# Group mean of y taken off by the product that turns y back to token order, and the centred tile copied by ScalarE, in a macaron block on one core

## The chip, the core and the metric

The kernel runs on one core of one Trainium2 chip. The time is device microseconds (us) of one execution of the whole program. The engines are TensorE (PE in the profile; its weight loads are PEld), VectorE (DVE), ScalarE (ACT), GpSimd (POOL) and SyncE (SP), which issues the DMAs. Each engine works through its own instructions in the order in which they are written, and waits on semaphores for the others.

## What is computed

The input x is 1024 tokens by 256 channels, all fp32. The block is x + 0.5 ffn(layernorm(x)), then + retention(layernorm(x)), then + 0.5 ffn(layernorm(x)) again. The change lies in the retention part:

```python
y = jnp.einsum('bhts,bhsd->bhtd', scores, v)
yg = y.transpose(0, 2, 1, 3).reshape(B * T, H, D)        # H = 16 groups of D = 16
mu = jnp.mean(yg, axis=-1, keepdims=True)
var = jnp.var(yg, axis=-1, keepdims=True)
yn = (yg - mu) / jnp.sqrt(var + EPS)
yn = yn.reshape(B * T, C) * gn_weight[None] + gn_bias[None]
out = jax.nn.silu(x @ w_g) * yn
return out @ w_proj
```

Each token has 16 groups of 16 neighbouring channels, and each group loses its own mean.

## The kernel before

The tokens are cut into 8 chunks of 128 (NT = 8), the channels into 2 halves of 128 (KC = 2). The first feed-forward part, the retention part and the second feed-forward part follow each other and overlap at their edges. No scheduler stands between the text and the chip: each engine has one block in which its steps are called in the order in which they run.

The retention part runs as a loop over c = 0 to 6, with the steps of several chunks in one iteration, and a written-out ending for chunk 7. On PE an iteration is: scores(c), project_out(c-3), project_vg(c+1), turn_h2(c+2), values(c, 0), turn_gn(c-2), values(c, 1), turn_qk(c+1), turn_y(c-1), project_qk(c+2), update_state(c+1). The ending is turn_h(2), turn_y(6), scores(7), project_out(4), values(7, 0), values(7, 1), turn_gn(5), turn_y(7), gate_up(12) and so on; gate_up starts the second feed-forward part. So turn_y(0) to turn_y(5) are called in the loop, and turn_y(6) and turn_y(7) behind it.

For one chunk the group norm goes through these steps:

- PE's values (L1107, L1101) leaves y in PSUM with the channels in partitions; ACT's copy_y (L458) copies it to yT in SBUF.
- PE's turn_y (L1140) turns it to token order by two transposes of 128x128 into the first 256 columns of bank 7 (bank 5 for chunk 7).
- DVE's group_mean sums each group (gsum, L735) and subtracts gsum/16 from the turned tile (gd, L739, into SBUF; gd has two buffers).
- ACT's square (L465) makes gsq, DVE's group_var (L747) sums it to gvar, POOL's group_roots makes gve (L320) and the power -0.5, grstd (L324), DVE's group_norm (L753) makes gn.
- PE's turn_gn (L1153) turns gn into the other half of the same bank, ACT's affine (L473) makes ga, DVE's gated (L761) go, PE's project_out (L1163) the product, and DVE's add_proj (L765) adds it to x1.

Other names in the rows: turn_qk is L1068, project_qk L1042, update_state L1120, scores L1085, project_vg L1053 and L1056, turn_h2 L1030, turn_h L961, gate_up L986. ACT's copy_qk makes kT (L446), qM (L448, two instructions) and qT (L452); copy_v makes v (L433) and sg (L437). DVE's rotate_parts makes rc and rs (L695), mask_kv kvm (L725), mask_scores sc (L715, four instructions), rotate rot (L707, L708), fuse_up fuse (L660), norm_tile h (L632), rest_h hh (L644).

Two guards matter for the order. turn_y(c) writes the bank from which the centred tile of the chunk before is read, so turn_y(6) waits for gd_done of chunk 5; turn_gn(c) and project_out(c) wait for gd_done of later chunks that share the bank. The constants (identity, causal mask, group mask and two columns) come in one tile msk by one DMA, which SP issues behind the first weight pieces and the first half of x.

Of the kernel before, what the change touches and what calls it, by code (L numbers as in the profile page):

```python
# [27 lines left out]
ALU = mybir.AluOpType  # L28
# [75 lines left out]
def masks():  # L104

    p = np.arange(P)
    return np.concatenate([
        np.eye(P), p[:, None] <= p[None, :], p[:, None] // D == p[None, :] // D,
        (p[:, None] // D) % 2 == np.arange(2)[None, :],
    ], 1).astype(np.float32)  # L110


def macaron(nc, x, w_qkv, w_g, w_proj, gn_w, gn_b, gate_w, up_w, down_w, gate_s, up_s, down_s,
            rotation_t, mask_t, out):
    with ExitStack() as ctx:
        def sb(name, shape, dt=F32):
            return ctx.enter_context(nc.sbuf_tensor(name, shape, dt))

        def sem(name):
            return ctx.enter_context(nc.semaphore(name))  # L120
# [11 lines left out]
        msk = sb("msk", [P, 3 * P + 2])  # L132
# [28 lines left out]
        gsum = sb("gsum", [P, H])  # L161
# [15 lines left out]
        ident, causal, own = msk[:, 0:P], msk[:, P:2 * P], msk[:, 2 * P:3 * P]  # L177
        gate_col, up_col = vec[:, 0:NI], vec[:, NI:2 * NI]
# [12 lines left out]
        def packed(ring, q):  # L191
# [39 lines left out]
        yT_done, y_turned, gsum_done, gd_done, gsq_done, gvar_done, gve_done, grstd_done, gn_done = (  # L231
            sem(n) for n in ("yT_done", "y_turned", "gsum_done", "gd_done", "gsq_done", "gvar_done", "gve_done",
# [143 lines left out]
        def _(act):  # L376
# [16 lines left out]
            def split_h(g, k):  # L393

                act.wait_ge(turned, (g if g < NG else g + NG) * TH + TH)
                if g >= NG:
                    act.wait_ge(up_done, NG * NI)
                nc.scalar.activation(hhi[:, k, g % NG, :], turn[g][k][:, :], ACT.Copy).then_inc(hhi_done, 1)
# [61 lines left out]

            def square(c):
                act.wait_ge(gd_done, c + 1)
                if c >= 1:
                    act.wait_ge(gvar_done, c)
                nc.scalar.activation(gsq[:, :], gd[:, c % 2], ACT.Square).then_inc(gsq_done, 1)  # L465
# [61 lines left out]
            for c in range(NT - 1):  # L527
                if c >= 2:
                    square(c - 2)
                copy_v(c + 1)  # L530
                if c + 2 < NT:
                    copy_h2(c + 2)
                if c >= 2:
                    affine(c - 2)
                copy_y(c)
                copy_qk(c + 1)
            c, j0 = NT - 1, NG * NI
            square(c - 2)
            split_h(2, 0)
# [3 lines left out]
            affine(c - 2)  # L543
            square(c)
# [23 lines left out]
        def _(dve):  # L568
# [162 lines left out]
            def group_mean(c):  # L731
                dve.wait_ge(y_turned, c + 1)
                if c >= 1:
                    dve.wait_ge(gd_done, c)
                dve.tensor_reduce(gsum[:, :], per_head(b_turned_y[c][:, 0:C]), AX.X, ALU.add).then_inc(gsum_done, 1)  # L735
                dve.wait_ge(gsum_done, c + 1)
                if c >= 2:
                    dve.wait_ge(gn_done, c - 1)
                dve.scalar_tensor_tensor(out=per_head(gd[:, c % 2]), in0=gsum[:, :].unsqueeze(2).to_broadcast([P, H, D]),  # L739
                                         scalar=-1.0 / D, in1=per_head(b_turned_y[c][:, 0:C]),  # L740
                                         op0=ALU.mult, op1=ALU.add).then_inc(gd_done, 1)

# [114 lines left out]
            for c in range(NT - 1):  # L857
# [21 lines left out]
                if c >= 1:  # L879
                    group_mean(c - 1)  # L880
# [6 lines left out]
            group_mean(c - 1)  # L887
# [8 lines left out]
            group_mean(c)  # L896
# [42 lines left out]
        def _(pe):  # L939
# [184 lines left out]
            def turn_y(c):  # L1124
# [14 lines left out]
                for k in range(KC):  # L1139
                    mm = pe.transpose(b_turned_y[c][:, k * P:(k + 1) * P], yT[:, c % 2, k, :], ident)  # L1140
# [142 lines left out]
```

## Time and profile before

| what | value |
|---|---|
| median of 3 runs | 173.49 us (173.36 to 173.67) |
| the profiled execution | 173.6 us |
| its span, first to last instruction | 171.8 us |
| mean granted TensorE clock | 0.999 |
| PE, DVE, ACT, POOL busy | 161.0, 137.1, 75.9, 68.9 us |

The span is 1.8 us shorter than the time of the same execution. A row of the timeline gives start, duration, engine, line, operation, output <- input, and how often it stands there in a row; square brackets give the engine's idle time before it and what ended that. The chain of waits is followed back from the last instruction; in it a PE row lasts only until the next instruction of PE starts, so its numbers are the pace at which PE moves on. In the timeline a PE row holds the whole pipeline of its last instruction too, and rows overlap.

### The profile page before, as it was taken

The numbers are of one execution on the slowest core, as the hardware profiler recorded it, in microseconds if no ns is written. First come the engines' busy times: TensorE is split into PE (matmuls) and PEld (weight loads), VectorE is DVE, ScalarE is ACT, GpSimd is POOL, SyncE is SP. The second block draws the span as 40 slices with busy tenths as digits, with TensorE's granted clock in tenths as the row PEclk, the third lists the DMA queues.
The fourth block names the chain that finished last, engine by engine and source line by source line (L and its number), as shares of the span: only waits on it lengthen the run. The fifth ranks groups of instructions, "written<-read, shape, count | busy, mean of one in ns | idle before, by whom it ended". The sixth has DMA issues, their size and how long they took to land.

```text
span 171.8 us, 3264 instructions
## 1 busy us (share of the span) xinstructions
PE 161.0 (94%) x1125; PEld 123.1 (72%) x1125; DVE 137.1 (80%) x294; ACT 75.9 (44%) x162; POOL 68.9 (40%) x76
## 2 busy tenths in 40 slices
PE   5996998989989999999999999999899999999992
PEld 2454766678969786768686777867666788898881
DVE  2799989999847266869797979998887899666763
ACT  3145398869402306161707062534716646225600
POOL 2354295425580611117474746465297530000000
PEclk9999999999999999999999999999999999999999
DMA  4999203803000000000000000000000000011002
GB/s 155 277 352 310 84 2 64 306 0 120 4 0 0 4 0 0 4 0 0 6 0 4 2 0 0 4 0 6 0 0 2 0 4 0 0 61 61 6 31 92
DMA packets 6848, 8.41 MB, mean 49 GB/s; under 512 B 416, under 2 KB 5552, under 8 KB 6832
## 3 DMA queue, kind: packets, MB, share of 16 engines
q1 hardware_dynamic: 6832, 8.20, 14.9%
q8 instruction: 9, 0.15, 0.4%
q14 instruction: 7, 0.06, 0.1%
HBM read 7.15 MB, written 1.05 MB: 48 GB/s over the span
## 4 chain that ended last, share of the span: by engine, by line
PE 62%; DVE 19%; issue 7%; POOL 6%; DMA 3%; ACT 2%; SPq 0%; POOLq 0%; DVEq 0%
PE bank L986 18%; PE bank L1014 10%; PE bank L1042 7%; PE bank L1107 5%; POOL grstd L324 3%; PE bank L1053 3%; PE bank L1085 3%; PE bank L1056 3%; PE bank L1163 3%; DVE h L632 3%; DMA xt<-in_L_attn_x 3%; PE bank L1068 2%; DVE fuse L660 2%; DVE sc L715 2%; DVE grid L574 2%
## 5 line engine op out<-in xcount | busy, mean ns | idle before, releaser
L986 PE MATMUL bank<-hh,gate_r 128*128 128x512 f32 x96 | 27.6, 407 | 2.5 <-DVE hh L644 1.0
L986 PE MATMUL bank<-hh,up_r 128*128 128x512 f32 x96 | 26.3, 396 | 0.0
L1014 PE MATMUL bank<-down_r,fhi 128*128 128x256 f32 x96 | 24.3, 291 | 0.3 <-DVE flo L668 0.3
L324 POOL TENSOR_TENSOR grstd<-gve,neg_half 128x16 f32<-128x16 f32 x8 | 23.3, 2917 | 0.7
L1014 PE MATMUL bank<-down_r,flo 128*128 128x256 f32 x96 | 23.4, 282 | 0.0
L408 ACT ACTIVATE gact<-bank,vec 128x512 f32<-128x512 f32 x24 | 16.4, 685 | 14.9 <-PE bank L986 14.6
L986 PEld LDWEIGHTS bank<-hh,gate_r 128*128 128x128 f32 x96 | 16.8, 188 | 8.0 <-issue 3.7
L660 DVE SCALAR_TENSOR_TENSOR fuse<-bank,vec,gact 128x512 f32<-128x512 f32 x24 | 17.9, 745 | 4.1 <-PE bank L986 3.9
L986 PEld LDWEIGHTS bank<-hh,up_r 128*128 128x128 f32 x96 | 18.1, 188 | 4.3
L715 DVE TENSOR_TENSOR sc<-bank,msk 128x512 f32<-128x512 f32 x32 | 19.8, 680 | 0.0
L433 ACT ACTIVATE v<-bank 128x256 f32<-128x256 f32 x8 | 3.1, 384 | 37.0 <-PE bank L1056 37.0
L1014 PEld LDWEIGHTS bank<-down_r,fhi 128*128 128x128 f32 x96 | 18.1, 188 | 1.5 <-DVE flo L668 1.0
L1014 PEld LDWEIGHTS bank<-down_r,flo 128*128 128x128 f32 x96 | 18.1, 188 | 0.5 <-issue 0.2
L416 ACT ACTIVATE fhi<-fuse 128x512 fp32r<-128x512 f32 x24 | 14.9, 629 | 6.8 <-DVE fuse L660 6.8
L1042 PE MATMUL bank<-wqkv,h 128*128 128x512 f32 x32 | 15.1, 594 | 0.0
L668 DVE TENSOR_TENSOR flo<-fuse,fhi 128x512 fp32r<-128x512 f32 x18 | 13.3, 744 | 0.8 <-ACT fhi L416 0.7
L678 DVE TENSOR_TENSOR yd<-bank,ds 128x256 f32<-128x256 f32 x16 | 6.7, 422 | 8.5 <-PE bank L1014 8.4
L1107 PE MATMUL bank<-sc,v 128*32 128x128 f32 x256 | 13.1, 279 | 0.0
L300 POOL TENSOR_SCALAR ve<-mv 128x1 f32<-128x1 f32 (+3 forms) x14 | 3.8, 272 | 23.0 <-DVE mv L607 22.9
L293 POOL TENSOR_TENSOR grid<-raw,grid 128x256 f32<-128x256 f32 (+2 forms) x6 | 7.7, 1290 | 12.3 <-DVE raw L586 12.3
L308 POOL TENSOR_TENSOR flo<-fuse,fhi 128x512 fp32r<-128x512 f32 x6 | 9.6, 1611 | 4.9 <-ACT fhi L416 4.9
L302 POOL TENSOR_TENSOR rstd<-ve,neg_half 128x1 f32<-128x1 f32 (+3 forms) x14 | 10.0, 715 | 1.2
(80 smaller groups left out, 300.0 us busy)
## 6 DMA issues: line engine op xcount, KB each, us to landing
raw<-in_rotation SPq DMA_DIRECT2D x1, 1536.0 KB, 7.1
xt<-in_L_attn_x SPq DMA_DIRECT2D x2, 512.0 KB, 5.4
out<-xt SPq DMA_DIRECT2D x8, 128.0 KB, 1.7
raw<-in_L_ffn_down_w SPq DMA_DIRECT2D x2, 384.0 KB, 8.2
wqkv<-in_L_attn_w_qkv SPq DMA_DIRECT2D x1, 768.0 KB, 9.6
raw<-in_rotation SPq DMA_DIRECT2D x1, 512.0 KB, 3.5
raw<-in_L_ffn_gate_w SPq DMA_DIRECT2D x1, 384.0 KB, 7.2
raw<-in_L_ffn_up_w SPq DMA_DIRECT2D x1, 384.0 KB, 7.7
```

What stands on the lines that cost most here:

```text
L302: pool.tensor_tensor(rstd[:, a:b], ve[:, a:b], neg_half[:, 0:b - a], ALU.pow).then_inc(rstd_done, 1)
L308: pool.tensor_tensor(flo[:, g % NG, i, :], fuse[:, j % FUSE_SLOTS, :], fhi[:, g % NG, i, :].bitcast(F32), ALU.subtract).then_inc(flo_pool, 1)
L324: pool.tensor_tensor(grstd[:, c % 2], gve[:, :], neg_half[:, :], ALU.pow).then_inc(grstd_done, 1)
L408: nc.scalar.activation(gact[:, j % 2, :], pairs[j // (NG * NI)][j % 2][0][:, :], ACT.Silu, scale=gate_col[:, i:i + 1]).then_inc(silu_done, 1)
L416: nc.scalar.activation(fhi[:, g % NG, i, :], fuse[:, j % FUSE_SLOTS, :], ACT.Copy).then_inc(fhi_done, 1)
L660: dve.scalar_tensor_tensor(out=fuse[:, j % FUSE_SLOTS, :], in0=pairs[j // (NG * NI)][j % 2][1][:, :], scalar=up_col[:, i:i + 1], in1=gact[ ...
L668: dve.tensor_tensor(flo[:, g % NG, i, :], fuse[:, j % FUSE_SLOTS, :], fhi[:, g % NG, i, :].bitcast(F32), ALU.subtract).then_inc(flo_dve, 1)
L715: dve.tensor_tensor(sc[:, r].rearrange("p k m t -> p (k m) t"), b_sc[r][:, :].rearrange("p (g t) -> p g t", t=P), causal.unsqueeze(1).to_b ...
L986: mm = pe.matmul(dst[:, :], wr[m][:, k * I + i * P:k * I + (i + 1) * P], half[:, k, g % NG, :], start=(k == 0 and half is hhi), stop=(k == ...
L1014: mm = pe.matmul(downs[d][:, 0:C], half[:, g % NG, i, t * P:(t + 1) * P], wr["down"][:, i * C:(i + 1) * C], start=(i == 0 and half is fhi) ...
L1042: mm = pe.matmul(b_qk[:, :], h2[:, c % 2, k, :], wqkv[:, k, 0:2 * C], start=(k == 0), stop=(k == KC - 1))
L1107: mm = pe.matmul(b_y[r * 2 * D:(r + 1) * 2 * D, k * P:(k + 1) * P], v2[:, c % 2, hd, :], sc[:, r, k, m, :], start=(c == 0 and m == 0), sto ...
```

## The change

The constant tile gets a fourth 128x128 matrix, named centre: identity minus 1/16 wherever row and column belong to one group. turn_y multiplies yT by it (an ordinary fp32 product) where it was transposed with the identity, so that the turned tile comes out with each group's mean taken off. DVE's group_mean and the tile gsum go. ACT's new step copy_centred copies the turned, centred tile from PSUM to gd; it is called at the end of each iteration of the loop and twice in the ending.

```diff
 def masks():
         (p[:, None] // D) % 2 == np.arange(2)[None, :],
+        np.eye(P) - (p[:, None] // D == p[None, :] // D) / D,
...
-        msk = sb("msk", [P, 3 * P + 2])
+        msk = sb("msk", [P, 4 * P + 2])
...
+        centre = msk[:, 3 * P + 2:]
...
+            def copy_centred(c):
+                act.wait_ge(y_turned, c + 1)
+                if c >= 2:
+                    act.wait_ge(gn_done, c - 1)
+                    act.wait_ge(gsq_done, c - 1)
+                nc.scalar.activation(gd[:, c % 2], b_turned_y[c][:, 0:C], ACT.Copy).then_inc(gd_done, 1)
...
                 copy_y(c)
                 copy_qk(c + 1)
+                if c >= 1:
+                    copy_centred(c - 1)
             c, j0 = NT - 1, NG * NI
             square(c - 2)
+            copy_centred(c - 1)
             split_h(2, 0)
             split_h(2, 1)
             square(c - 1)
             copy_y(c)
             affine(c - 2)
+            copy_centred(c)
             square(c)
...
-            def group_mean(c):
-                dve.wait_ge(y_turned, c + 1)
-                if c >= 1:
-                    dve.wait_ge(gd_done, c)
-                dve.tensor_reduce(gsum[:, :], per_head(b_turned_y[c][:, 0:C]), AX.X, ALU.add).then_inc(gsum_done, 1)
-                dve.wait_ge(gsum_done, c + 1)
-                if c >= 2:
-                    dve.wait_ge(gn_done, c - 1)
-                dve.scalar_tensor_tensor(out=per_head(gd[:, c % 2]), in0=gsum[:, :].unsqueeze(2).to_broadcast([P, H, D]),
-                                         scalar=-1.0 / D, in1=per_head(b_turned_y[c][:, 0:C]),
-                                         op0=ALU.mult, op1=ALU.add).then_inc(gd_done, 1)
...
                     gated(c - 2)
-                if c >= 1:
-                    group_mean(c - 1)
...
             c, j0 = NT - 1, NG * NI
-            group_mean(c - 1)
             group_var(c - 2)
...
             rest_h(2, 1)
-            group_mean(c)
...
                 for k in range(KC):
-                    mm = pe.transpose(b_turned_y[c][:, k * P:(k + 1) * P], yT[:, c % 2, k, :], ident)
+                    mm = pe.matmul(b_turned_y[c][:, k * P:(k + 1) * P], yT[:, c % 2, k, :], centre, start=True, stop=True)
                 mm.then_inc(y_turned, 1)
```

The order of PE's steps is the same in both kernels. ACT, at the end of an iteration of the loop (here c = 5) and the start of the next, before the change:

```order
L446 ACTIVATE kT<-bank 128x256 [waits sc_done,qk_turned]
L448 ACTIVATE qM<-bank,msk 128x2x128 x2
L452 ACTIVATE qT<-bank 128x256 [waits y_half]
L465 ACTIVATE gsq<-gd 128x256 [waits gvar_done,gd_done]
L433 ACTIVATE v<-bank 128x8x2x16 [waits y_half,kv_done,vg_done]
```

The same place after the change, where line numbers have moved:

```order
L447 ACTIVATE kT<-bank 128x256 [waits sc_done,qk_turned]
L449 ACTIVATE qM<-bank,msk 128x2x128 x2
L453 ACTIVATE qT<-bank 128x256 [waits y_half]
L467 ACTIVATE gd<-bank 128x256 [waits gsq_done,gn_done,y_turned]
L473 ACTIVATE gsq<-gd 128x256 [waits gvar_done,gd_done]
L434 ACTIVATE v<-bank 128x8x2x16 [waits y_half,kv_done,vg_done]
```

The copy to gd stands between the copies of q and k and the square; before, gd came from DVE, beside those copies.

DVE, from the last norm tile of the loop to the masks of chunk 7 and the norm of chunk 5, before the change:

```order
L632 TENSOR_SCALAR h<-x,mv,rstd 128x256 [waits turned,rstd_done]
L761 TENSOR_TENSOR go<-ga,sg 128x256 [waits proj_done,sg_done,ga_done]
L735 TENSOR_REDUCE gsum<-bank 128x16 [waits gd_done,y_turned]
L739 SCALAR_TENSOR_TENSOR gd<-gsum,bank 128x256 [waits gn_done,gsum_done]
L735 TENSOR_REDUCE gsum<-bank 128x16 [waits gd_done,y_turned]
L739 SCALAR_TENSOR_TENSOR gd<-gsum,bank 128x256 [waits gn_done,gsum_done]
L747 TENSOR_REDUCE gvar<-gsq 128x16 [waits gve_done,gsq_done]
L715 TENSOR_TENSOR sc<-bank,msk 128x512 [waits y_half,sc_done] x4
```

The same place after the change:

```order
L644 TENSOR_SCALAR h<-x,mv,rstd 128x256 [waits turned,rstd_done]
L761 TENSOR_TENSOR go<-ga,sg 128x256 [waits proj_done,sg_done,ga_done]
L747 TENSOR_REDUCE gvar<-gsq 128x16 [waits gve_done,gsq_done]
L727 TENSOR_TENSOR sc<-bank,msk 128x512 [waits y_half,sc_done] x4
L747 TENSOR_REDUCE gvar<-gsq 128x16 [waits gve_done,gsq_done]
```

The sum of squares of chunk 5 (the first gvar) now stands right behind go, with the four instructions for the means of chunks 5 and 6 gone from ahead of it.

ACT in the ending, after the change:

```order
L473 ACTIVATE gsq<-gd 128x256 [waits gvar_done,gd_done]
L467 ACTIVATE gd<-bank 128x256 [waits gsq_done,gn_done,y_turned]
L399 ACTIVATE hh<-bank 128x512 [waits up_done,turned] x2
L473 ACTIVATE gsq<-gd 128x256 [waits gvar_done,gd_done]
L459 ACTIVATE yT<-bank 128x256 [waits y_turned,y_half]
L481 ACTIVATE ga<-bank,vec 128x128 [waits go_done,gn_turned]
L467 ACTIVATE gd<-bank 128x256 [waits gsq_done,gn_done,y_turned]
```

Before the change the same stretch read gsq, hh twice, gsq, yT, ga; the copies of chunks 6 and 7 are put between these.

## Rows read from the trace of the kernel before

**Rows 1.** The page: busy time, share of the span, instructions

```profile
PE 161.0 (94%) x1125; PEld 123.1 (72%) x1125; DVE 137.1 (80%) x294; ACT 75.9 (44%) x162; POOL 68.9 (40%) x76
```

**Rows 2.** Busy time in one iteration: PE, PEld, DVE, ACT, POOL, clock, DMA, GB/s

```profile
93.44:102.52 9.08, 9.08 (x87) 6.80 (x86) 7.78 (x18) 3.82 (x12) 4.93 (x5) 1.00 0.00 1
```

**Rows 3.** Chain of waits (start, us, what): one iteration, pace of PE's steps

```profile
91.41 0.37 PE bank L1153 x2
...
92.60 0.58 PE bank L1068 x4
93.19 0.22 PE bank L1140 x2
93.40 1.72 PE bank L1042 x4
95.12 0.45 PE bank L1120 x4
```

**Rows 4.** Groups by line: what goes from DVE, and ACT's copy from PSUM

```profile
L735 DVE TENSOR_REDUCE gsum<-bank 128x16 f32<-128x256 f32 x8 | 3.4, 422 | 3.8 <-PE bank L1140 3.8
L739 DVE SCALAR_TENSOR_TENSOR gd<-gsum,bank 128x256 f32<-128x256 f32 x8 | 3.4, 421 | 0.3
...
L458 ACT ACTIVATE yT<-bank 128x256 f32<-128x256 f32 x8 | 3.1, 384 | 6.8 <-PE bank L1107 6.5
```

**Rows 5.** Timeline: ACT and DVE in one iteration of the loop

```profile
94.21 0.39 ACT L452 ACTIVATE qT<-bank 128x256 f32<-128x256 f32 x1
...
94.94 0.42 DVE L747 TENSOR_REDUCE gvar<-gsq 128x16 f32<-128x256 f32 x1 [0.30 <-ACT gsq L465]
95.28 0.68 DVE L695 TENSOR_TENSOR rc<-bank,raw 128x512 f32<-128x512 f32 x1
...
99.49 0.38 ACT L433 ACTIVATE v<-bank 128x256 f32<-128x256 f32 x1 [4.58 <-PE bank L1056]
...
99.53 0.41 DVE L753 TENSOR_TENSOR gn<-gd,grstd 128x256 f32<-128x256 f32 x1
...
100.42 0.20 PEld L1153 LDWEIGHTS bank<-msk,gn 128*128 128x128 f32 x2 [0.20 <-issue]
```

**Rows 6.** Timeline: the ending up to the second values of chunk 7

```profile
121.41 0.39 ACT L452 ACTIVATE qT<-bank 128x256 f32<-128x256 f32 x1
...
122.17 0.41 PE L1140 MATMUL bank<-msk,yT 128*128 128x128 f32 x2 [0.70 <-issue]
...
122.51 1.15 PE L1085 MATMUL bank<-qM,kT 32*128 32x256 f32 x16
...
123.41 0.41 DVE L747 TENSOR_REDUCE gvar<-gsq 128x16 f32<-128x256 f32 x1
123.74 2.48 DVE L715 TENSOR_TENSOR sc<-bank,msk 128x512 f32<-128x512 f32 x4
...
126.13 0.41 DVE L747 TENSOR_REDUCE gvar<-gsq 128x16 f32<-128x256 f32 x1
...
127.28 0.20 POOL L320 TENSOR_SCALAR gve<-gvar 128x16 f32<-128x16 f32 x1 [0.16 <-POOL grstd L324]
```

**Rows 7.** Timeline: where TensorE waits for the norm of chunk 6

```profile
127.56 3.00 POOL L324 TENSOR_TENSOR grstd<-gve,neg_half 128x16 f32<-128x16 f32 x1
...
128.66 1.16 PE L986 MATMUL bank<-hh,gate_r 128*128 128x512 f32 x4
...
131.08 0.44 PE L1153 MATMUL bank<-msk,gn 128*128 128x128 f32 x2 [0.32 <-DVE gn L753]
```

**Rows 8.** Chain of waits: pace of a pair of gate and up products

```profile
135.86 1.86 PE bank L986 x8
```

**Rows 9.** DMA issues: out<-in, KB each, us to landing

```profile
msk<-in_masks SPq DMA_DIRECT2D x1, 193.0 KB, 4.4
```

**Rows 10.** Timeline: TensorE waits for DVE at the start

```profile
9.06 0.13 PEld L1173 LDWEIGHTS bank<-msk,rows 16*128 16x128 f32 x1 [0.76 <-issue]
...
11.37 1.08 PE L961 MATMUL bank<-msk,h 128*128 128x128 f32 x6 [0.37 <-DVE h L632]
```

More of the change, by code:

```diff
@@ L160, in macaron @@
         yT = sb("yT", [P, 2, KC, P])
-        gsum = sb("gsum", [P, H])
         gd = sb("gd", [P, 2, C])
@@ L230, in macaron @@
             sem(n) for n in ("sc_done", "sc_masked", "y_half", "kv_done", "kvm_done", "state_done"))
-        yT_done, y_turned, gsum_done, gd_done, gsq_done, gvar_done, gve_done, grstd_done, gn_done = (
-            sem(n) for n in ("yT_done", "y_turned", "gsum_done", "gd_done", "gsq_done", "gvar_done", "gve_done",
+        yT_done, y_turned, gd_done, gsq_done, gvar_done, gve_done, grstd_done, gn_done = (
+            sem(n) for n in ("yT_done", "y_turned", "gd_done", "gsq_done", "gvar_done", "gve_done",
                              "grstd_done", "gn_done"))
```

## The prediction, made before the changed kernel ran

> **What bounds the kernel now.** I read the busy shares first [rows 1]: TensorE is busy for 94% of the span, VectorE 80%, ScalarE 44%. A share of the whole doesn't say what one step is worth, so I then asked for the busy time of one iteration of the retention loop [rows 2]. There TensorE is busy 9.08 us of 9.08, VectorE 7.78 and ScalarE 3.82. The reader is to see that the two engines which the change relieves and loads both have slack in the loop, and the third has none. The chain of waits says the same in another way [rows 3]: through the loop it runs over TensorE alone, one step ending where the next begins, and turn_y is one of these steps. From this follows the frame of the whole estimate: a step on TensorE counts in full in the loop, one on VectorE or ScalarE counts only if it makes TensorE wait. Behind the loop, from 111 to 135 us, this is different: there TensorE waits several times [rows 6, 7], and I go through these waits one by one. Behind 135.4 us the chain is again TensorE's, until the last product of gate and up.
>
> **The product in the place of the transpose.** The two transposes of one turn_y move TensorE on by 0.22 us, 0.11 each [rows 3]. An fp32 product of the same shape stands in the same iteration: update_state multiplies a 128x128 tile by 128 columns, twice. In the chain that is x4 and 0.45 us, where the two transposes were x2 and 0.22 [rows 3]. So an fp32 product is two instructions of TensorE at the pace of one transpose each, and the new turn_y should stand in the trace as x4 and 0.45: 0.22 us more. That holds at both ends of the pace, since both rows are read back to back in a busy stretch.
> In the loop turn_y is called six times. Five of them (chunks 0 to 4) are followed by project_qk without a wait: 5 x 0.22 = **+1.10 us**. The sixth is followed by turn_h and then by turn_y(6), where TensorE was idle for 0.70 us [rows 6]; that idle time takes it.
> The Trainium skill speaks against the change more strongly. Its page "TensorE: Matmul & The Clock Gate", section Terms, calls the transpose mode four times as fast for FP32. By that rule the new turn_y would take 0.88 us, and the five would cost 3.3 us and not 1.1. The rows of this case show two times, and the sum goes by them.
>
> **VectorE's mean.** Eight times 422 + 421 ns go [rows 4], 6.7 us of VectorE's work. In the loop this is worth nothing by itself, because TensorE doesn't wait for VectorE there: gn ends at 99.94 and TensorE loads it at 100.42 [rows 5]. In the ending it can matter (below).
>
> **ScalarE's copy.** It reads PSUM and writes 128x256 in SBUF, as the copy to yT does in 384 ns [rows 4]: 8 x 0.38 = 3.1 us on an engine that then waits 4.58 us for the next chunk's v [rows 5]. Its place is what has to be followed. It is queued behind qT, which starts at 94.21 and takes 0.39 [rows 5]. One after the other, qT, the copy (0.38) and the square (taken like a copy) bring gvar to 94.21 + 0.39 + 0.38 + 0.38 = 95.36, or 0.1 us less or more for overlaps and semaphores. Before, it was at 94.94. TensorE's own 0.22 us delays everything behind turn_y, but not the q and k copies ahead of it; against TensorE's next steps gvar is thus late by 0.42 - 0.22 = 0.2 us. Queued behind gvar on VectorE are rc, rs, the mask of kv and the four masks of scores, then gn and rot. All move by the same 0.2 us, since gvar gave way to rc within 0.34 us before. The nearest user is turn_gn: gn had 0.48 us in hand [rows 5], of which 0.28 remain. I take nothing for the loop. If the cover were gone, TensorE would wait once per iteration from c = 2 to 5.
> The waits that copy_centred adds are on y_turned, which turn_y sets at about 93.19 + 0.45 = 93.64 [rows 3], 0.9 us before the copy's turn, and on gn and gsq of earlier chunks, which are an iteration old.
>
> **The ending.** Times here are on the clock of before, shifted by the 1.10 us.
> turn_y(6) waited until gd of chunk 5 was there (122.17) [rows 6]. The copy to gd is queued behind qT, which starts at 121.41: it ends at 121.41 + 0.39 + 0.38 = 122.18 at the latest, so turn_y(6) starts where it did, and the sixth 0.22 is absorbed. It is longer itself, so scores(7) start 0.2 later. They took until 123.66, and the masks began at 123.74 [rows 6]: now 123.9. **+0.2 us**, for values(7) wait for these masks.
> turn_y(7) is longer too, **+0.22 to 0.25**. So gate_up(12), at 128.66 before [rows 7], starts at 129.1.
> Then comes the join with the norm of chunk 6. Before, the power on GpSimd for this chunk ended at 130.56 and turn_gn(6) started at 131.08 [rows 7]. A pair of gate and up products takes 1.86 [rows 8], so TensorE had come to that point at 130.52 and stood for 0.56 us (0.32 in the row, which counts the end of the pipeline; that is the other bound). Now gvar of chunk 5 no longer waits for the means of 5 and 6 on VectorE (123.41 before [rows 6]; now one more 0.38 behind the copy, about 122.6), so GpSimd's power for chunk 5 ends before gvar of chunk 6 arrives. That one stands behind the masks, at 126.3 and not 126.13; gve, which began at 127.28 behind the previous power [rows 6], begins at 126.8, the power ends at about 130.1, and turn_gn(6) could start at 130.6. TensorE arrives at 129.1 + 1.86 = 130.96. The wait is gone and TensorE itself is next: 130.96 against 131.08 is **-0.12 us** for the ending as a whole, +0.12 by the other bound. The last join, gn of chunk 7, is gated by fuse on VectorE behind gate_up(13), so it follows TensorE.
>
> **The start.** The tile msk grows by 128 x 128 x 4 bytes = 64 KB. Its DMA took 4.4 us for 193 KB [rows 9]; in proportion that would be at most 1.5 us more. The first use is at 9.06, and TensorE then waits for h from VectorE at 11.37 all the same [rows 10]. I take 0, since that wait lies between; the upper bound would leave up to 1 us.
>
> **The sum.** +1.10 for the loop, -0.12 for the ending, 0 for the start: +1.0 us. The profiled execution took 173.6 with a span of 171.8, so I expect a span of 172.8 and 174.6 for such an execution. The median of the runs is 0.1 below it: **174.5 us**.
>
> **Rivals.**
> *The loop now waits for the group norm as well.* If the chain qT, copy, gsq, gvar is slower than I put it (0.5 us against TensorE where I put 0.2), gn comes 0.2 to 0.25 us too late for turn_gn in four iterations, and the ending is later by as much: +1.0 + 0.9 = about 175.5. For it speaks that only 0.28 us remain. Against it, that each of the four durations has its row.
> *Freed VectorE pays: the kernel gets faster.* turn_gn advances TensorE by 0.37 where two transposes need 0.22, and turn_qk by 0.58 for four where 0.44 would do [rows 3]. If these gaps came from VectorE's queue, a VectorE with 0.84 us less per iteration would close them; with the like of project_out some 0.5 us in each of four iterations, 2.0 - 1.0: 172.5. It decides from 0.25 us per iteration on. Against it: gn was ready 0.48 us before its use [rows 5], and the profile names no releaser for the gap.
> *It costs nothing that can be measured.* The ending gives back 0.7 us more: the power of chunk 6 ends 0.5 earlier, and if gate_up(12) weren't in front of turn_gn(6), that would reach the end. Then +0.3 or less: 173.8. Against it: the order of TensorE's steps is fixed, and gate_up(12) is ahead.
> *The product costs four transposes.* That is the skill's rule, worked as a mechanism of this kernel: 0.66 us for each of the five, and 1.3 in the ending less the 0.56 wait: +4.0, 177.6. Against it stands update_state with its own row [rows 3].
>
> **How the numbers follow.** A difference of 0.2% (0.35 us) is about what can be told from no change here. My forecast (between +0.6 and +1.4) gets 0.68, the late norm 0.12, four transposes 0.02, no measurable change 0.10, faster 0.08. Slower by over 0.2% is thus 0.82, within it 0.10, faster 0.08. The forecast's own spread is the ending's 0.25 us, the pace (0.22 or 0.23) and some 0.2 us at the start. The range has to take in the late norm at the top, and comes down to just where a change can't be measured at the bottom: 173.8 to 175.6.
>
> **What would show it.** Right: turn_y as x4 and 0.45 in the chain, x32 in all, an iteration of 9.30 us with TensorE full; gvar about 0.2 us later against rc's producer; the second power in the ending about 0.5 us earlier, and TensorE's 0.32 us before turn_gn(6) gone. Wrong: a wait of TensorE on gn inside the loop; an iteration of 9.08 or less; turn_h's products at 11.37 later by more than 0.1 us.

## The result, and the profile after

The changed kernel takes 174.34 us (median of 7 runs, 174.19 to 184.25), the kernel before 172.99 us in the same comparison. The ratio is 1.0071, 95% interval 1.0049 to 1.0092: slower, by 1.2 us. Forecast were 174.5 us and +1.0 us against the kernel before. That the time itself lies so near the forecast is in part luck: the kernel before took 172.99 us here, where the forecast started from 173.49, and the loss was larger than forecast.

The profiled execution of that comparison ran at a granted clock of 0.856 and took 184.25 us; it is left out of the ratio, as three executions of 389 to 855 us are in the comparisons further down. The rows below are from a second run of the same changed kernel with a clock of 1.000 (174.32 us, span 172.5). Its page first: busy time, share of the span, instructions.

```profile
PE 162.1 (94%) x1141; PEld 124.7 (72%) x1141; DVE 131.5 (76%) x278; ACT 79.0 (46%) x170; POOL 69.5 (40%) x76
```

Beside [rows 1]: TensorE has 16 instructions more (eight turn_y's with two more each) and 1.1 us more busy time, VectorE 16 instructions and 5.6 us less, ScalarE 8 instructions and 3.1 us more. VectorE is relieved by five times what TensorE is loaded with, and the kernel is slower.

Where it went shows in the busy time of two iterations of the loop (columns as in [rows 2]: the stretch, then PE, PEld, DVE, ACT, POOL). The first is the second iteration, the other a full one, each from one project_qk to the next.

```profile
75.25:84.22 8.97, 8.97 (x87) 6.63 (x85) 6.36 (x15) 4.21 (x13) 5.15 (x5) 1.00 0.01 2
93.53:102.84 9.31, 9.31 (x91) 7.04 (x89) 7.04 (x16) 4.21 (x13) 5.20 (x6) 1.00 0.01 3
```

The full iteration is 9.31 us where it was 9.08 [rows 2]. TensorE shows no idle time in either; a wait shorter than the 0.28 us that a row of one product lasts doesn't show as idle time, as the second iteration will tell. The chain of waits of the changed kernel in a full iteration answers [rows 3]:

```profile
91.47 0.37 PE bank L1149 x2
...
92.66 0.59 PE bank L1064 x4
93.25 0.45 PE bank L1136 x4
93.69 1.72 PE bank L1038 x4
95.41 0.45 PE bank L1116 x4
```

turn_y (L1136) is now x4 and 0.45, to the digit what update_state (L1116) is. The other steps are as they were, the 0.37 of turn_gn and the 0.59 of turn_qk included.

I measured all kernels in the same way, since the starts of TensorE's steps repeat to 0.02 us between two profiles of one kernel. The table has the iterations from the start of one project_qk to that of the next, their sum, and the time from the last project_qk to turn_gn(7), behind which every kernel has 36.4 us left. The first start counted is that of project_qk(2), the first one that the loop calls; the iteration named the second is that of c = 2, and the last iteration of the loop, c = 6, lies in the ending.

| kernel | iterations, us | sum | ending |
|---|---|---|---|
| before, two profiles | 8.29, 8.54, 9.08, 9.08, 9.08 | 44.07 | 24.02 |
| changed, two profiles | 8.52, 8.97, 9.31, 9.31, 9.31 | 45.42 | 23.96 |
| product_alone | 8.51, 8.69, 9.31, 9.31, 9.31 | 45.13 | 24.30 |
| copy_alone | 8.29, 8.97, 9.08, 9.08, 9.08 | 44.50 | 23.85 |
| v_centred | 8.29, 8.97, 9.07, 9.08, 9.08 | 44.49 | 23.84 |
| product_square_first, two profiles | 8.52, 8.69, 9.31, 9.31, 9.31 | 45.14 | 23.83 |
| v_square_first, two profiles | 8.29, 8.52, 9.08, 9.08, 9.08 | 44.05 | 23.40 |
| reduced_product | 8.24, 8.97, 9.08, 9.09, 9.08 | 44.46 | 23.92 |
| double_copy | 8.52, 9.24, 9.36, 9.35, 9.35 | 45.82 | 24.50 |

The changed kernel loses 1.35 us in the loop and gets 0.06 back in the ending: 1.29 us. Four of the five iterations lose 0.23 each. The second loses 0.43, and that is the one thing the forecast did not have.

How well whole times can be told apart has to be said once. The span of one kernel varies by 0.9 us between executions (before: 171.0 to 171.9 in one comparison, with one at 172.5), and the loop's first project_qk, project_qk(2), of the same changed kernel starts at 66.73 in one profile and 67.18 in another. The two profiles of before, at 67.33 and 67.27, happen to be late ones, which is why the profiled spans differ by only 0.7 us. And the kernel before, run as a kernel of its own, came out at 1.0015 (1.0005 to 1.0025) times itself. So a ratio says little below 0.2%, and the verdicts below rest on the table.

In the second iteration the steps between project_vg and turn_gn show the loss. The chain of the changed kernel:

```profile
80.60 0.24 PE bank L1026 x2
80.84 0.42 PE bank L1097 x2
81.27 0.90 PE bank L1103 x15
82.16 0.37 PE bank L1149 x2
```

and of the kernel before in the same place:

```profile
80.97 0.22 PE bank L1030 x2
81.19 0.22 PE bank L1101 x2
81.41 0.92 PE bank L1107 x15
82.33 0.37 PE bank L1153 x2
```

values(2, 0), L1107 before and L1103 now, needs 0.59 us in a full iteration. Here it took 0.92 before the change already: TensorE was waiting for VectorE's masks inside the group. In the changed kernel the step ahead of it (L1097) is stretched from 0.22 to 0.42 as well. What ends the wait is the last of the four masks. The masks and the turn_gn behind the values, in the timeline of the kernel before:

```profile
79.18 2.47 DVE L715 TENSOR_TENSOR sc<-bank,msk 128x512 f32<-128x512 f32 x4
...
82.26 0.44 PE L1153 MATMUL bank<-msk,gn 128*128 128x128 f32 x2
```

and of the changed kernel:

```profile
77.14 0.42 DVE L747 TENSOR_REDUCE gvar<-gsq 128x16 f32<-128x256 f32 x1 [1.83 <-ACT gsq L473]
...
79.01 2.47 DVE L727 TENSOR_TENSOR sc<-bank,msk 128x512 f32<-128x512 f32 x4
...
82.09 0.44 PE L1149 MATMUL bank<-msk,gn 128*128 128x128 f32 x2
```

In both, turn_gn starts 0.61 us behind the end of the masks. Counted from project_qk (75.62 and 75.25) the masks are 0.20 us later in the changed kernel, and so is turn_gn; the other 0.23 is turn_y's. The iteration c = 2 has no project_out (1.06 us in a full one), so less of TensorE's work stands between the scores and the values that need their masks.

The ending, in the timeline of the changed kernel, answers [rows 6, 7]:

```profile
122.36 0.40 ACT L467 ACTIVATE gd<-bank 128x256 f32<-128x256 f32 x1
...
122.87 0.68 PE L1136 MATMUL bank<-msk,yT 128*128 128x128 f32 x4 [0.48 <-issue]
...
123.25 0.42 DVE L747 TENSOR_REDUCE gvar<-gsq 128x16 f32<-128x256 f32 x1 [1.27 <-ACT gsq L473]
...
127.88 2.90 POOL L325 TENSOR_TENSOR grstd<-gve,neg_half 128x16 f32<-128x16 f32 x1
...
129.40 0.71 PE L1136 MATMUL bank<-msk,yT 128*128 128x128 f32 x4
129.87 1.18 PE L982 MATMUL bank<-hh,gate_r 128*128 128x512 f32 x4
...
131.82 0.38 PE L1149 MATMUL bank<-msk,gn 128*128 128x128 f32 x2
```

turn_y(6) waits until ScalarE's copy of chunk 5 is there, where it waited for VectorE's gd of chunk 5 before. turn_gn(6) at 131.82 has no idle time in brackets, where it had 0.32 [rows 7]: TensorE comes to it directly from gate_up(12). The power for chunk 6 ends at 130.78, and 0.75 us (how much later this profile is at its last project_qk) has to be taken off to compare: 130.03 where it was 130.56.

### The profile page after: what moved, and what is told of

Same layout as the page of the kernel before. It is cut to its first block, busy times and chain, and to the rows that moved or that the text cites. A ratio compares the mean times of both kernels' runs of the same rounds, so it can differ in the third digit from the quotient of the medians.

```text
span 182.4 us, 3281 instructions
## 1 busy us (share of the span) xinstructions
PE 174.7 (96%) x1141; PEld 130.1 (71%) x1141; DVE 132.0 (72%) x278; ACT 78.9 (43%) x170; POOL 68.3 (37%) x76
## 4 chain that ended last, share of the span: by engine, by line
PE 81%; DVE 12%; issue 2%; DMA 2%; ACT 1%; SPq 0%
PE bank L982 22%; PE bank L1010 11%; PE bank L1038 9%; PE bank L1103 7%; PE bank L1081 5%; PE bank L1049 5%; PE bank L1052 4%; PE bank L1159 4%; PE bank L1064 3%; PE bank L1136 2%; DVE h L644 2%; PE bank L1097 2%; DMA xt<-in_L_attn_x 2%; PE bank L1116 2%; DVE grid L586 2%
## 5 line engine op out<-in xcount | busy, mean ns | idle before, releaser
L982 PE MATMUL bank<-hh,gate_r 128*128 128x512 f32 x96 | 29.3, 428 | 1.5 <-DVE hh L656 0.7
L982 PE MATMUL bank<-hh,up_r 128*128 128x512 f32 x96 | 28.1, 417 | 0.0
L1010 PE MATMUL bank<-down_r,fhi 128*128 128x256 f32 x96 | 25.6, 301 | 0.2 <-DVE flo L680 0.2
L1010 PE MATMUL bank<-down_r,flo 128*128 128x256 f32 x96 | 24.6, 290 | 0.0
L982 PEld LDWEIGHTS bank<-hh,gate_r 128*128 128x128 f32 x96 | 17.4, 194 | 7.7 <-issue 2.8
L1010 PEld LDWEIGHTS bank<-down_r,fhi 128*128 128x128 f32 x96 | 18.8, 196 | 1.2 <-DVE flo L680 0.4
L1010 PEld LDWEIGHTS bank<-down_r,flo 128*128 128x128 f32 x96 | 18.8, 196 | 0.7 <-issue 0.3
L1038 PE MATMUL bank<-wqkv,h 128*128 128x512 f32 x32 | 17.4, 675 | 0.0
L1103 PE MATMUL bank<-sc,v 128*32 128x128 f32 x256 | 13.0, 293 | 0.0
L747 DVE TENSOR_REDUCE gvar<-gsq 128x16 f32<-128x256 f32 x8 | 3.3, 418 | 10.8 <-ACT gsq L473 10.8
```

Source lines behind the costliest of these rows:

```text
L982: mm = pe.matmul(dst[:, :], wr[m][:, k * I + i * P:k * I + (i + 1) * P], half[:, k, g % NG, :], start=(k == 0 and half is hhi), stop=(k == ...
L1010: mm = pe.matmul(downs[d][:, 0:C], half[:, g % NG, i, t * P:(t + 1) * P], wr["down"][:, i * C:(i + 1) * C], start=(i == 0 and half is fhi) ...
L1038: mm = pe.matmul(b_qk[:, :], h2[:, c % 2, k, :], wqkv[:, k, 0:2 * C], start=(k == 0), stop=(k == KC - 1))
L1103: mm = pe.matmul(b_y[r * 2 * D:(r + 1) * 2 * D, k * P:(k + 1) * P], v2[:, c % 2, hd, :], sc[:, r, k, m, :], start=(c == 0 and m == 0), sto ...
```

## The experiments

**The changed kernel again**, for the profile used above.

> The changed kernel once more, for a profile at the full granted clock. Theory: 1.0 us slower than before (0.6 to 1.3), the span 1.0 longer; turn_y at a pace of 0.44 to 0.45 us, an iteration of the loop at 9.30 with TensorE full, 1.10 us lost by the end of turn_y(4), and 0.1 given back behind it. Rival (the norm is late in the loop): TensorE waits on gn before turn_gn in four iterations, and an iteration takes 9.5 or more.

Measured: ratio 1.0054 (1.0036 to 1.0072), the iterations of the table. The pace and the ending came as said, the loss in the loop did not stop at 1.10. The rival, a wait on gn in four iterations, is out: gn has the 0.28 us in hand that the prediction left it. VectorE's timeline and TensorE's load in the full iteration behind 93.53:102.84:

```profile
109.32 0.42 DVE L753 TENSOR_TENSOR gn<-gd,grstd 128x256 f32<-128x256 f32 x1
...
110.02 0.20 PEld L1149 LDWEIGHTS bank<-msk,gn 128*128 128x128 f32 x2 [0.20 <-issue]
```

**The product alone.** On the kernel before:

```diff
-                    mm = pe.transpose(b_turned_y[c][:, k * P:(k + 1) * P], yT[:, c % 2, k, :], ident)
+                    mm = pe.matmul(b_turned_y[c][:, k * P:(k + 1) * P], yT[:, c % 2, k, :], ident, start=True, stop=True)
```

> The kernel before with turn_y as an fp32 product with the identity; VectorE keeps the mean and ScalarE copies nothing more. It computes the same. Theory (only the steps in the loop pay in full, the ending's join hides part): five times 0.22 in the loop, and 0.22 in the ending, where the extra of turn_y(6) delays everything and that of turn_y(7) disappears in the wait for the norm of chunk 6: 1.3 us slower than before. Rival (every turn_y pays): 8 x 0.22 = 1.8 us. Rival (VectorE's freed time is what mattered): no more than the changed kernel, 1.0.

Measured: ratio 1.0070 (1.0046 to 1.0094), 1.2 us; in the table +1.06 in the loop and +0.28 in the ending, 1.34. The five steps in the loop pay, of the three others about one does. Not every turn_y pays (1.8 us would be 1.0104), and VectorE's freed time was not what mattered: with its mean kept, the kernel is as slow as the changed one. The second iteration takes only 0.15 more here, since part of the 0.22 goes into the wait for the masks that stood there already: turn_gn starts 0.61 us behind the masks here too, and these come 3.47 us behind project_qk, where it was 3.56.

**The copy alone.** On the changed kernel, the transposes back:

```diff
-                    mm = pe.matmul(b_turned_y[c][:, k * P:(k + 1) * P], yT[:, c % 2, k, :], centre, start=True, stop=True)
+                    mm = pe.transpose(b_turned_y[c][:, k * P:(k + 1) * P], yT[:, c % 2, k, :], ident)
```

> The changed kernel with the two transposes put back in turn_y: ScalarE copies the turned tile, VectorE has no mean, and nothing takes the group's mean off (the output differs by that); the larger constant tile stays. Theory: nothing in the loop; in the ending gvar of chunk 5 comes 0.8 us earlier, the power of chunk 6 ends about 0.5 us earlier, and turn_gn(6) follows gate_up(12) directly: 0.5 us faster than before. Rival (freed VectorE closes gaps of TensorE in the loop): 2 us faster. Rival (the copy on ScalarE is late): not faster than before.

Measured: ratio 1.0019 (0.9991 to 1.0046). I had expected 0.5 us less than before, and the table has 0.26 more. It also says where. The ending's join gave the 0.5 us as forecast (turn_gn(6) 2.14 us behind turn_y(7), where it was 2.64), but the second iteration lost 0.43 and the last one 0.37. Rows of this kernel in the second iteration: masks, and the values which wait for them.

```profile
79.17 2.48 DVE L727 TENSOR_TENSOR sc<-bank,msk 128x512 f32<-128x512 f32 x4
...
81.22 1.10 PE L1103 MATMUL bank<-sc,v 128*32 128x128 f32 x16
```

Project_qk started at 75.18 here and at 75.62 before, the masks at 79.17 and 79.18: counted from project_qk they are 0.43 us later, exactly what the iteration lost. In the last iteration it is gn that TensorE waits for. The way there is a detour over GpSimd: the masks of c = 5 are late without holding TensorE up, and behind them in VectorE's queue stand the statistics for the next norm tiles (0.43 us later against project_qk). GpSimd's rstd comes later by as much, and the norm tiles, which wait for it, stand ahead of gvar:

```profile
112.75 1.06 DVE L644 TENSOR_SCALAR h<-x,mv,rstd 128x256 f32<-128x256 f32 x3 [1.09 <-POOL rstd L303]
113.73 0.41 DVE L747 TENSOR_REDUCE gvar<-gsq 128x16 f32<-128x256 f32 x1
...
118.31 0.41 DVE L753 TENSOR_TENSOR gn<-gd,grstd 128x256 f32<-128x256 f32 x1
...
118.78 0.20 PEld L1149 LDWEIGHTS bank<-msk,gn 128*128 128x128 f32 x2 [0.31 <-DVE gn L753]
```

So the copy on ScalarE has a price of its own, though ScalarE is idle for 54% of the span. In the changed kernel the longer turn_y hides half of it: gvar comes 2.12 us behind project_qk in the copy alone, 1.89 in the changed kernel and 1.70 before, so that only 0.2 are lost in the second iteration. The last one even gets 0.07 back (turn_y(5) 8.75 us behind project_qk, where it was 8.82): with the means gone, the norm tiles start 0.91 and not 1.00 us behind project_qk there, and gvar behind them 1.90 and not 1.97. This is the one place in the loop at which the freed VectorE pays.

**The square ahead of the copy.** If late gvar is the cause, an earlier gvar must take it away. On the changed kernel, for chunks 0 to 4:

```diff
             def square(c):
-                act.wait_ge(gd_done, c + 1)
+                if c < NT - 3:
+                    act.wait_ge(y_turned, c + 1)
+                    src = b_turned_y[c][:, 0:C]
+                else:
+                    act.wait_ge(gd_done, c + 1)
+                    src = gd[:, c % 2]
...
-                nc.scalar.activation(gsq[:, :], gd[:, c % 2], ACT.Square).then_inc(gsq_done, 1)
+                nc.scalar.activation(gsq[:, :], src, ACT.Square).then_inc(gsq_done, 1)
...
-                if c >= 2:
-                    square(c - 2)
                 copy_v(c + 1)
...
+                if 1 <= c < NT - 2:
+                    square(c - 1)
                 if c >= 1:
                     copy_centred(c - 1)
...
             def group_norm(c):
                 dve.wait_ge(grstd_done, c + 1)
+                dve.wait_ge(gd_done, c + 1)
```

> The changed kernel, with ScalarE's square of chunks 0 to 4 taken straight from the turned tile in PSUM and put ahead of the copy to gd, so that gvar comes 0.4 us earlier; the same is computed. Theory (late gvar pushes VectorE's masks, and TensorE's values of chunk 2 wait for them): the second iteration takes 8.76 us in the place of 8.97, the others 9.31 as before, and the kernel is 0.2 us faster than the changed one, 0.9 to 1.1 slower than before. Rival (the wait in that iteration comes from elsewhere): it stays at 8.97 and the time doesn't move.

Measured first: ratio 1.0064 (1.0048 to 1.0079). The trace says what was expected and a little more: the second iteration fell from 8.97 to 8.69, the value of the product alone, and the ending from 23.96 to 23.83. The chain of the second iteration of this kernel:

```profile
80.59 0.22 PE bank L1032 x2
80.81 0.22 PE bank L1103 x2
81.03 0.84 PE bank L1109 x16
```

The stretched step is back at 0.22, and turn_gn comes 0.61 us behind the end of the masks here too. But the changed kernel was not measured beside it, and its earlier ratio of 1.0054 is no worse, so both were run again on one chip.

> The changed kernel a third time, beside the next two on one chip. Theory: 1.2 us slower than before (1.1 to 1.35), iterations 8.52, 8.97, 9.31, 9.31, 9.31.

> The same kernel as product_square_first, to have its time beside the changed kernel's on one chip. Theory (the 0.28 us which the trace shows gained in the second iteration and 0.13 in the ending are real time): 0.3 to 0.4 us faster than the changed kernel in the same call. Rival (they are given back in executions without this profile): no difference beyond 0.1.

Measured: the changed kernel 1.0079 (1.0063 to 1.0096), this one 1.0047 (1.0027 to 1.0066), 174.71 and 174.10 us. The difference is 0.6 us with an uncertainty of about 0.4; the table has 0.41. The iterations of both repeated to 0.01 us. The cause of the extra loss in the second iteration is shown: gvar's place in VectorE's queue ahead of the masks. The copy to gd is still there and takes as long; only what stood behind it has moved.

**A second copy.** The same cause from the other side: on the changed kernel,

```diff
+        spare = sb("spare", [P, C])
...
+                nc.scalar.activation(spare[:, :], b_turned_y[c][:, 0:C], ACT.Copy)
                 nc.scalar.activation(gd[:, c % 2], b_turned_y[c][:, 0:C], ACT.Copy).then_inc(gd_done, 1)
```

> The changed kernel with a second, useless copy of the turned tile on ScalarE ahead of the one to gd; the same is computed. It moves gvar another 0.3 us back. Theory (gn has about 0.28 us in hand in a full iteration of the changed kernel, the masks of chunk 2 none): the second iteration takes another 0.3 us (9.25 to 9.3), the full ones 9.31 to 9.40, since the slack just covers it, and the last one of the loop another 0.2 to 0.3. Together 0.6 us slower than the changed kernel. Rival (ScalarE's order is covered everywhere by its idle 4.4 us): no difference.

Measured: ratio 1.0127 (1.0107 to 1.0147), 0.9 us slower than the changed kernel on the same chip. The second iteration took 9.24 and the full ones 9.35 to 9.36, as expected: the second one has no slack and pays 0.27, the full ones pay 0.05, so their slack was 0.2 to 0.25 us for a delay of 0.27. The loss in the ending was put too low: it was 0.54 us, of which 0.28, as expected, before turn_y(5), and 0.27, which I had not counted, at turn_y(6), which waits for the copy of chunk 5:

```profile
121.93 1.04 PE L959 MATMUL bank<-msk,h 128*128 128x128 f32 x8
123.72 0.68 PE L1138 MATMUL bank<-msk,yT 128*128 128x128 f32 x4 [0.75 <-issue]
```

**A product without the price.** On the changed kernel yT and the matrix became fp32r:

```diff
-        yT = sb("yT", [P, 2, KC, P])
+        yT = sb("yT", [P, 2, KC, P], F32R)
+        centre_r = sb("centre_r", [P, P], F32R)
...
             split_f(11)
+            act.wait_ge(mask_in, 16)
+            nc.scalar.activation(centre_r[:, :], centre, ACT.Copy)
...
-                    mm = pe.matmul(b_turned_y[c][:, k * P:(k + 1) * P], yT[:, c % 2, k, :], centre, start=True, stop=True)
+                    mm = pe.matmul(b_turned_y[c][:, k * P:(k + 1) * P], yT[:, c % 2, k, :], centre_r[:, :], start=True, stop=True)
```

> The changed kernel with yT and the matrix as fp32r (one instruction for each product, y rounded to fewer bits by ScalarE's copy; this changes the precision of y). The matrix is copied once on ScalarE. Theory: the products pace TensorE no slower than transposes (0.06 to 0.11 us each), so the 0.22 per turn_y go and what is left is what the copy alone showed: iterations 8.29, 8.97, 9.08, 9.08, 9.08, no more than 0.2 us from before. Rival (the weight load of 190 ns paces it): 0.2 us per pair, the same as transposes.

Measured: ratio 1.0015 (1.0003 to 1.0027), which is what the kernel before has against itself. The chain gives the pace of the two steps:

```profile
93.06 0.17 PE bank L1139 x2
93.23 1.77 PE bank L1041 x4
```

0.17 for the pair, and project_qk behind it 0.05 longer than 1.72: together the 1.94 of a transposed pair. Whether the products or the loads of their weights set this pace the run doesn't settle; 0.17 to 0.22 fits the theory and the rival. The iterations are within 0.05 us those of the copy alone, the loss in the second one included. With TensorE's price gone, what the copy costs and what the ending gives back nearly cancel: the table has 0.29 us more than before.

**The mean taken off the weights.** y is linear in v, and v in its weights, so the group mean can be taken off the value weights once. On the copy alone (without the larger constant tile):

```diff
+            def centre_weights():
+                dve.wait_ge(wqkv_in, 16)
+                for k in range(KC):
+                    dve.tensor_reduce(wsum[:, k, :], per_head(wqkv[:, k, 2 * C:3 * C]), AX.X, ALU.add).then_inc(wsum_done, 1)
+                dve.wait_ge(wsum_done, KC)
+                for k in range(KC):
+                    dve.scalar_tensor_tensor(out=per_head(wqkv[:, k, 2 * C:3 * C]),
+                                             in0=wsum[:, k, :].unsqueeze(2).to_broadcast([P, H, D]),
+                                             scalar=-1.0 / D, in1=per_head(wqkv[:, k, 2 * C:3 * C]),
+                                             op0=ALU.mult, op1=ALU.add).then_inc(wv_done, 1)
...
             scale_down(3)
+            centre_weights()
             rotate_parts(0)
...
                     pe.wait_ge(wg_in, 16)
+                    pe.wait_ge(wv_done, KC)
```

> The transposes stay and ScalarE copies the turned tile, but the mean is taken off the value weights: once, before the first use, VectorE subtracts from the value columns of wqkv the mean of each group of 16 columns (four instructions of 128x256 between scale_down(3) and the first rotation, where it was idle for 2.66 us). y is linear in v, so y comes out centred and the same result is computed. Theory: as the copy alone, 0.5 us faster than before, with the four instructions (4 x 0.42 less overlaps, 1.5 us) hidden in that idle time. Rival: they delay the first v product or the first rotation by up to 1 us, and it is no faster than before.

> The value weights centred once, the transposes kept, and the square ahead of the copy; the same is computed. Theory: both losses of the copy alone go (0.43 us in the second iteration, 0.37 in the last one), what stays is the 0.5 us which the ending gives back: iterations 8.29, 8.54, 9.08, 9.08, 9.08, 8.82 and 0.5 us faster than before. Rival: VectorE is at its limit in the second iteration anyway, and no more than 0.2 us are gained over before.

> The same kernel as v_square_first. Theory: span 0.5 us shorter than before, time 0.2 to 0.3 us shorter, because this kernel spends 0.3 us more outside its span than the others. Rival: the extra 0.3 us outside the span were an accident of one load, and the time is 0.5 us shorter.

Measured: v_centred 1.0028 (1.0008 to 1.0047), not faster, with the iterations of the copy alone. The four new instructions are hidden; VectorE still waits for project_qk(0) behind them:

```profile
48.60 0.73 DVE L746 TENSOR_REDUCE wsum<-wqkv 128x16 f32<-128x256 f32 x2
49.37 0.88 DVE L749 SCALAR_TENSOR_TENSOR wqkv<-wsum,wqkv 128x256 f32<-128x256 f32 x2
51.34 0.69 DVE L707 TENSOR_TENSOR rc<-bank,raw 128x512 f32<-128x512 f32 x1 [1.09 <-PE bank L1050]
```

With the square ahead of the copy both losses went, as the table shows: loop 44.05, ending 23.40, 0.64 us less than before. Its spans agree (medians 170.8 and 170.9 in two comparisons, before 171.3 and 171.4). Its times do so less: 0.9984 (0.9972 to 0.9996) and 0.9994 (0.9975 to 1.0013), because this kernel spends 2.16 and 2.12 us outside its span, v_centred 2.04, and every other kernel 1.77 to 1.81. That is the same in both comparisons, so it is no accident of one load. Why it is so stays open; it was not tried apart. This is the best version found, with the full mathematics and the transposes, and the gain of its time over the kernel before (0.16 and 0.06%) is no larger than the 0.15% that the kernel before has against itself.

**The kernel before again.**

> The kernel before once more, to have its profile beside the others of this chip. Theory: the iterations of the loop take 8.29, 8.54, 9.08, 9.08, 9.08 us from one project_qk to the next, as in its first profile, and what differs from that profile lies ahead of the loop. Rival: the iterations themselves vary by 0.2 us from run to run, so that the 0.43 us of the changed kernel's second iteration mean nothing.

Measured: ratio 1.0015 (1.0005 to 1.0025), iterations 8.29, 8.55, 9.08, 9.08, 9.08 and ending 24.02, like the first profile. The iterations don't vary from run to run, so the 0.43 us mean something; what varies lies ahead of the loop. It starts with when the first half of x has landed: 4.3 us after its issue in both profiles of before, 3.6 to 4.0 in several of the other kernels. The chain of waits of before begins with this landing, and so does that of double_copy, the earliest one:

```profile
1.20 4.32 DMA xt<-in_L_attn_x
```

```profile
1.21 3.62 DMA xt<-in_L_attn_x
```

It landed 0.70 us earlier, and project_qk(2) starts 0.70 us earlier (66.63 and 67.33). The others whose chain begins with it lie between, on the same line to 0.1 us (3.86 and 66.89, 3.99 and 67.05, 4.20 and 67.25). In three profiles the chain begins with the landing of the first gate weights, and project_qk(2) starts at 66.72 to 66.79. So what varies ahead of the loop is mostly when these first transfers land. Since project_qk(2) of one and the same kernel varied by 0.45 us as well, I don't count this for or against the change.

## Why the prediction was right, and where it was not

- **The frame** (a step of TensorE counts in full in the loop, work of VectorE and ScalarE only where TensorE waits for it) held. VectorE lost 5.6 us of work, and all that TensorE got for it by the end of the loop is the 0.07 us in the last iteration.
- **The product's price** was +1.10 for five steps. Measured are 0.23 in each of four iterations and 0.15 to 0.22 in the second: +1.06 with the product alone. Taking the price from update_state's row and not from a rule was right. The Trainium skill's statement (page "TensorE: Matmul & The Clock Gate", section Terms) that the transpose mode is four times as fast for FP32 would, by the estimate in the prediction, have given 0.88 for a turn_y, where the trace has 0.45. The trace decides: at this shape the pace of a transpose is twice that of a product.
- **The copy on ScalarE in the loop** was taken at nothing. Here the prediction failed at one step. It put gvar 0.2 us late against TensorE, and that is what came: 1.89 us behind project_qk in the second iteration, where it was 1.70. It put the slack of gn at 0.28, and that came too. But "the nearest user is turn_gn" was wrong for the second iteration, where the values stand closer behind the masks and TensorE was already waiting for them. That wait stood in the trace of before, as a group of values of 0.92 us beside 0.59 in a full iteration; I had read one full iteration and taken it for all. The term put at nothing is 0.20 us against before. Against the product alone, whose earlier gvar had shortened the wait, the copy costs 0.28.
- **The ending** was put at -0.12 (bound +0.12), and was -0.06. The mechanism is right: turn_y(6) starts where it did (1.97 behind turn_y(5), before 1.95), turn_y(7) came 6.53 behind it, where it was 6.27 (0.2 was forecast, 0.26 came), and turn_gn(6) follows gate_up(12) with no wait, 2.42 behind turn_y(7). The number is in part luck: from turn_y(6) to turn_gn(6) it took 8.95 us where it was 8.91, +0.04 and not -0.12, since turn_gn(6) starts 1.95 behind gate_up(12), where 1.86 was put, and 0.06 more came ahead of turn_y(7). What made it -0.06 all the same are two terms that the forecast didn't have, 0.07 in the last iteration and 0.05 between turn_gn(6) and turn_gn(7).
- **The start** was taken at 0. No loss from the larger constant tile shows: its DMA took 4.2 to 4.6 us with 257 KB and 4.2 to 4.5 with 193 KB, so the bound of 1.5 us in proportion to its size was far off, and the changed kernel's project_qk(2) starts at 66.73 and 67.18, before at 67.33 and 67.27.
- **The sum** was +1.0; the traces have +1.29, the three comparisons 0.9 to 1.4 us. Of the 0.25 us that the loop lost beyond its 1.10, 0.20 is the missing term and 0.05 the 0.23 for 0.22; the ending's 0.06 is the rest.
- **The rivals.** "The loop now waits for the group norm as well" was a step in the right direction, with the wrong place: not gn in four iterations but the masks in one. "Freed VectorE pays" is out as a gain of 2 us: the 0.37 and 0.59 of turn_gn and turn_qk did not move with 0.74 us less on VectorE in a full iteration (7.04 where it was 7.78; the 0.84 of the prediction added up durations that overlap), and only the last iteration gained 0.07. "Nothing that can be measured" is what the copy alone and the fp32r product showed, not the change. "Four transposes" is out.

## What to carry to other kernels

Where one engine is busy without a gap, taking 6 us from another and giving it 0.2 us per step costs the sum of the steps: price the step by the nearest row of the same kind and shape, and look for the gain only at the places where the full engine waits. An idle engine is no cover for what is put into its queue: ask what is queued behind the next consumer, and look at every iteration of a loop, since the first ones have fewer steps and less slack. And where the operand is a product with constant weights, a linear correction can be made to the weights once and not to each tile.

## What the runs showed of the hardware

- A 128x128 fp32 product with 128 columns advances TensorE by 0.22 us in two instructions, a transpose of the same tile by 0.11 in one, an fp32r product by 0.08 to 0.11 (with the 0.05 that the step behind it lost). Each at a granted clock of 1.00. What sets the pace of the last two was not tried apart.
- Inside the retention loop the starts of TensorE's steps repeat to 0.02 us between executions of one kernel, while whole spans vary by 0.9 us. Differences of 0.2 us can be read from stretches of the trace, and not from times. In ten of the thirteen profiles at the full clock the chain of waits begins with the landing of the first half of x, 3.6 to 4.3 us after its issue, and the loop starts earlier or later by as much, to 0.1 us.
- The same program, loaded twice, differed by 0.15% (0.05 to 0.25%).
- The two kernels that centre the weights spend 2.04 to 2.16 us outside their span, the others 1.8. The cause stays open.
